# Expert weights in longer rows and fewer transfers, and a shorter warm-up, in a macaron block's kernel

## The reference

```python
x = x + 0.5 * ffn(layernorm(x), ...)
x = x + attn(layernorm(x), ...)
x = x + 0.5 * ffn(layernorm(x), ...)

def ffn(x):                                  # 64 experts, 6 per token, F = 192, H = 512
    topk_w, topk_ids = grouped_topk(x @ gate_w, bias)
    # per expert e, the first CAP of its tokens:
    h = silu(buf[e] @ w_gate[e]) * (buf[e] @ w_up[e])
    y[tokens of e] += topk_w * (h @ w_down[e])
    return y + silu(x @ ws_gate) * (x @ ws_up) @ ws_down
```

## Time and profile before

| | |
|---|---|
| median of 3 runs | 1313.1 us (1312.18 to 1315.88) |
| profiled execution | 1316.83 us, its span 1315.0 us |
| mean granted TensorE clock | 0.964 |
| busy: TensorE, VectorE, ScalarE, GpSimd | 1199.3, 614.9, 508.3, 526.3 us |
| moved by DMA | 288.73 MB in 180,972 packets |
| of that q1 (SP's queue) | 214.73 MB in 144,928 packets, 51.2% of sixteen engines over the span |
| q0 (GpSimd's queue) | 57.69 MB in 23,808 packets, 19.3% |

### The profile page before, as it was taken

One profiled execution on the slowest core, in us unless ns is written; L12 is line 12 of the kernel. 1 busy time (PEld: TensorE's weight loads), 2 busy tenths in 40 slices (PEclk: granted clock), 3 DMA queues, 4 the chain that ended last, 5 costly groups with the idle time before them and its releaser, 6 DMA issues.

```text
span 1315.0 us, 26511 instructions
## 1 busy us (share of the span) xinstructions
PE 1199.3 (91%) x10352; PEld 789.8 (60%) x10352; DVE 614.9 (47%) x1198; ACT 508.3 (39%) x1303; POOL 526.3 (40%) x417
## 2 busy tenths in 40 slices
PE   7998999999779889999999999999999999998770
PEld 5535777776557655665565565564437777776650
DVE  7791222222125677777777866643790222221120
ACT  2222111111113467888788778761122111111100
POOL 0113655555531654443434433100104555655533
PEclk9998999999999889999999999999999999999895
DMA  9989999999988533233423342230959999999977
GB/s 335 396 277 295 322 322 319 315 308 322 308 230 243 159 87 76 66 81 81 125 70 81 107 103 66 81 141 37 370 190 341 320 322 321 315 311 311 314 179 134
DMA packets 180972, 288.73 MB, mean 220 GB/s; under 512 B 21488, under 2 KB 103792, under 8 KB 180848
## 3 DMA queue, kind: packets, MB, share of 16 engines
q1 hardware_dynamic: 144928, 214.73, 51.2%
q0 software_dynamic: 23808, 57.69, 19.3%
q10 hardware_dynamic: 12112, 14.61, 3.2%
HBM read 210.15 MB, written 55.57 MB: 202 GB/s over the span
## 4 chain that ended last, share of the span: by engine, by line
PE 61%; DVE 13%; DMA 12%; issue 5%; ACT 4%; POOL 2%; SPq 1%; ACTq 0%; DVEq 0%; POOLq 0%
PE ps L386 15%; PE ps L402 9%; PE ps L462 5%; PE ps L504 4%; PE ps L516 4%; PE ps L482 4%; DMA out<-osb,tok 4%; DMA ya_d<-osb,tok 3%; DMA buf<-xn_d,tok 3%; PE ps L530 3%; PE ps L369 2%; PE ps L444 2%; PE ps L285 2%; PE ps L572 2%; DVE Mx L1200 2%
## 5 line engine op out<-in xcount | busy, mean ns | idle before, releaser
L386 PE MATMUL ps<-bufT,gu 128*64 128x96 f32 x6144 | 296.6, 258 | 20.0 <-issue 17.4
L386 PEld LDWEIGHTS ps<-bufT,gu 128*64 128x64 f32 x6144 | 286.6, 175 | 29.1 <-issue 18.3
L1200 DVE TENSOR_REDUCE Mx<-ps 128x1 f32<-128x512 f32 x256 | 170.8, 684 | 70.9 <-PE ps L482 64.6
L791 ACT ACTIVATE ps<-ps,Mx 128x512 f32<-128x512 f32 x256 | 175.4, 687 | 49.3 <-DVE Mx L1200 42.9
L402 PE MATMUL ps<-wd,h 64*96 64x512 f32 x768 | 182.5, 608 | 8.6 <-DVE osb L1113 8.3
L747 ACT COPY bufT<-ps 128x384 f32<-128x384 f32 x128 | 60.5, 477 | 312.7 <-PE ps L369 312.5
L806 ACT ACTIVATE PT<-ps 128x512 f32<-128x512 f32 x256 | 159.2, 623 | 50.7 <-PE ps L504 48.4
L1103 DVE TENSOR_TENSOR h<-sg,ps 128x288 f32<-128x288 f32 x64 | 29.1, 454 | 312.1 <-PE ps L386 312.1
L1347 POOL DMA_INDIRECT buf<-xn_d,tok x128 | 130.0, 1015 | 100.4 <-issue 57.5
L1113 DVE TENSOR_SCALAR osb<-ps,gt 96x512 f32<-96x512 f32 x128 | 89.9, 742 | 144.5 <-PE ps L402 144.5
L482 PE MATMUL ps<-St 96*128 96x512 f32 x252 | 117.3, 484 | 7.7 <-ACT ps L791 7.7
(11 more groups left out here) (162 smaller groups left out, 1685.2 us busy)
## 6 DMA issues: line engine op xcount, KB each, us to landing
gu<-in_L_ffn_w_gate SPq DMA_DIRECT2D x128, 384.0 KB, 10.2
gu<-in_L_ffn_w_up SPq DMA_DIRECT2D x128, 384.0 KB, 12.0
wd<-in_L_ffn_w_down SPq DMA_DIRECT2D x192, 256.0 KB, 10.5
St<-HL SPq DMA_DIRECT2D x186, 128.0 KB, 2.4
qkr<-in_L_attn_W_in SPq DMA_DIRECT2D x28, 256.0 KB, 3.4
X<-in_L_attn_X SPq DMA_DIRECT2D x4, 1024.0 KB, 11.2
ya_d<-X SPq DMA_DIRECT2D x4, 1024.0 KB, 18.2
yb_d<-XN ACTq DMA_DIRECT2D x16, 256.0 KB, 2.6
```

The source lines that it names most:

```text
L386: t = e.matmul(bk[64 * k:64 * k + 64, CAP * j:CAP * j + CAP], gu[:, 2 * k + m, c, j:F:3], f.bufT[(2 * q + k) % 4][:, c, :], start=(c == 0) ...
L791: e.activation(bk, bk, ACT.Exp, bias=Mx[:, qt, hl:hl + 1], accum_out=Dn[:, qt, hl:hl + 1]).then_inc(a_den, 1)
L1200: e.tensor_reduce(Mx[:, qt, hl:hl + 1], bank((4, 5, 7)[n % 3]), AX, ALU.max, negate=True).then_inc(a_max, 1)
```

## The change

`load_up` issues two transfers per pair in place of four, each of 256 rows of 3072 bytes in place of 1536. `load_down` issues one in place of three, of 128 rows of 6144 bytes in place of 2048. The counts of the two waits follow. `pe_busy` at the attention's head does 34 products in place of 45.

```diff
         def pe_gate_up(e, f, q):
-            e.wait_ge(s_gu[q % NR], loaded(f, 2 * q, 4))
+            e.wait_ge(s_gu[q % NR], loaded(f, 2 * q, 2))
         def pe_down(e, f, q):
-            e.wait_ge(s_dn[q % NR], loaded(f, 2 * q, 3))
+            e.wait_ge(s_dn[q % NR], loaded(f, 2 * q, 1))
             pe_experts(e, f1)
             e.wait_ge(f_h, E // 2)
-            pe_busy(e, 45)
+            pe_busy(e, 34)
         def load_up(e, f, q):
             gu = f.ring[q % NR][0]
             x = slice(2 * q, 2 * q + 2)
-            for c in (slice(0, 2), slice(2, 4)):
-                for m, w in enumerate((w_gate, w_up)):
-                    e.dma_start(gu[:, m::2, c, :], w[x].rearrange("x (p c) f -> p x c f", c=4)[:, :, c, :]).then_inc(s_gu[q % NR], 16)
+            for m, w in enumerate((w_gate, w_up)):
+                e.dma_start(gu[:, m::2, :, :], w[x].rearrange("x (p c) f -> p x c f", c=4)).then_inc(s_gu[q % NR], 16)
         def load_down(e, f, q):
-            for j in range(3):
-                e.dma_start(wd[:, j, :], w_down[x].rearrange("x (p j) h -> (x p) j h", j=3)[:, j, :]).then_inc(s_dn[q % NR], 16)
+            e.dma_start(wd[:, :, :], w_down[x].rearrange("x (p j) h -> (x p) j h", j=3)).then_inc(s_dn[q % NR], 16)
```

## The result

The changed kernel takes 1330.73 us (median of 4 runs, 1329.15 to 1333.52) against 1312.64 (4 runs, 1310.34 to 1315.88): ratio 1.0122, 95% interval 1.0102 to 1.0142. It is 1.2% **slower**; the prediction had said 1299 us and faster. (The quotient of the two medians is 1.0138. The ratios here are those on record, with their intervals.) The profiled execution took 1331.35 us, its span is 1329.5 against 1315.0 before.

A forecast was written before the change was run, and what follows sets the result against it. Bound: full DMA engines, with weight reloads and serial scatters both slower than TensorE. Gains of 7 us (first FFN), 4 (second) and 3 (warm-up), 14 off 1316.8, give 1303, less 3.7 for the median: 1299 us, range 1281 to 1331.

The forecast's parts named there:

- Both loops: In the FFNs: weight reloads, 10.6 us a pair to become 10.2, and GpSimd's serial scatters, about 8.6 us each.
- the late weights: Last gate/up products start 15.4 us late in the first FFN, 19.9 in the second; the second has 11.0 us of weight waits.
- ScalarE's wait: End of first FFN: 13.6 us waiting for the attention's first weights, expected to be gone.
- case A: The prediction's own case: weights gain, scatters lose, the loops trade; 1294 to 1306 us, chance 0.38.
- the lap: Time from one scatter's issue to the next: from about 8.6 us to 8.95; over 9.3 would be wrong.
- the row of turns: Each of a scatter's six rows per engine cedes to one weight row, 76 ns becoming 150: +0.45 us per lap.
- The second term: Before the experts: larger rows may delay ScalarE's stores and the first gathers, half a microsecond each.
- The free last laps: End of each FFN, loads over: the last scatters follow at 5.0 us each, to 391 and 1274 us.
- Warm-up: Attention's head: eleven fewer products gain 3 us, low bound 0; first cast 15 us behind the last scatter's landing.
- D: Rival, slower: a scatter's start waits behind weight rows in flight, lap 9.8 to 10.5; centre 1330 us, chance 0.28.
- B: Rival: turns are not by row, scatter laps stay 8.6 us; 1287 us, chance 0.20.
- C: Rival: nothing measurable, longer laps eat the weights' gain or rows are cut again; 1309 to 1317 us, chance 0.14.

The follow-up runs named there:

- w34: Kernel before with 34 warm-up products in place of 45 and nothing else: 1310.94 us, ratio 0.9981.
- down_one_short: Kernel before with down weights in one 768 KB transfer, rows still 2048 bytes, in six (second FFN five) of eight ring buffers: 1311.06 us, ratio 0.9994.
- gu_long: Kernel before with only gate and up weights in 3072-byte rows and two transfers: 1313.5 us, ratio 1.0000.
- both_mid: Kernel before with gate and up rows of 3072 bytes and down rows of 4096 and 2048 bytes: 1312.96 us, ratio 0.9994.
- down_long: Kernel before with only down weights changed, one transfer with 6144-byte rows: 1333.91 us, ratio 1.0137.
- after_start: Changed kernel with the short rows of before for the first eight pairs of each FFN: 1326.10 us, ratio 1.0100.
- down_long_i2: Kernel before with down weights in 6144-byte rows, two transfers each filling every second partition: 1325.35 us, ratio 1.0086.
- half: Kernel before with 34 warm-up products and gate and up rows of 3072 bytes from pair 16 on, down rows 2048: 1307.24 us, ratio 0.9958.

## Why the prediction was wrong

**What bounds the kernel**: right in its parts. Both loops are there, the weights' and the scatters', and the change did make the first faster and the second slower. SP was free early, the late weights and ScalarE's wait were gone, q1's packets came out to the last one, and the mean weight row was the 150 ns forecast. The time of 1330.7 us lies at the very end of the range, 1331, which the rivals had stretched so far; case A's own ended at 1306.

**The step that failed is the lap.** "I take a lap of 8.95"; measured 9.44 and 9.33, past the 9.3 that the prediction had named as its sign of being wrong. The term was sized at +0.45 us for six turns, less 0.1; it is +0.82 and +0.75. The prediction's own chain carries it to the result. Scatter 25 starts at 373.51 where 355.6 was forecast: 4.8 us are the first scatter's, 13 the 25 laps'. Pair 30 stands 14.0 us behind it, at 387.46 (13.5 forecast), and pair 31 7.2 behind that, at 394.63 (8 less 3 forecast). The last scatter follows 13.8 us later, at 408.45 where 391 stood. The second FFN repeats it: its first scatter 7.7 us late, 9.8 more by scatter 25 at 1255.97, and the last gate/up at 1278.84 where 1257 was forecast.

Why the lap was too small: the row of turns took a scatter as six turns, each the mean weight row, and left the time before its first row as it was. The single records of q0 in the traces (start and duration of each row; means of 17 laps in each FFN) show both parts. In three kernels with short rows (before, w34, down_one_short) the first row of a scatter is served 4.9 to 5.1 us after its issue and the last one 1.6 to 1.8 later; in the changed kernel it is 5.3 and 5.4, and then 2.1. A row of a scatter takes 176 ns in both kernels, so what grew is the time before and between them, 0.2 to 0.5 us of it before the first. The two queues from 1.6 to 4.7 us after the issue of a scatter, first the one of the earlier trace rows, then the changed kernel's at 249.50, show one thing that differs there: q0 is still busy with gathers issued earlier.

```profile
q1 hardware_dynamic: 660, 1.01, 96.0%
q0 software_dynamic: 30, 0.06, 7.5%
...
q1 hardware_dynamic: 152, 0.58, 62.8%
q0 software_dynamic: 105, 0.34, 38.6%
```

How much of the later start that is, is not shown. The 0.3 to 0.5 us within the six turns look like the forecast, but that is luck: in gu_long and both_mid, with mean rows of 111 and 129 ns, this part stays at 1.7 to 1.8, and in down_long, with 91, it is 1.9. The lap does not follow the mean row. It does follow the row's length, and 6144 bytes stand out. That the prediction chose the middle of an unknown cost by a rule that one stretch of 1536- and 2048-byte rows showed, and applied it to rows three times as long, is its error. Whether turns are by row, by packet or otherwise is still open.

**The second term is the start.** "Larger rows may delay ScalarE's stores and the first gathers, half a microsecond each"; the first scatter starts at 136.6 where six kernels with short rows at the start have 131.8 to 134.4, so 2 to 5 us, and after_start puts its worth at some 4 us, with the uncertainty said there.

**The free last laps** were counted nearly right, 21.2 us from scatter 27 to the last where 20 were forecast, but they came after a longer loop. Of what the loads gained nothing is left once the scatters set the pace.

**Warm-up**: right. The head's first cast stands 15.3 us behind the last landing. The chain of waits at the changed kernel's head (start us, us, what):

```profile
410.38 4.23 DMA yb_d<-osb,tok
...
429.94 0.44 DVE xT L1156
```

410.38 + 4.23 = 414.6, and 429.94 follows 15.3 later. Alone it is worth 0.2%, 2 to 3 us, at the edge of what was measured.

**The rivals.** D had the sign, 1330 and "it decides from a lap of about 9.3 on", and the laps were 9.33 and 9.44. Its mechanism, a start that waits behind a number of rows, asked for 3 us more before the first row and a lap of 9.8 at least. The start did grow, but by 0.2 to 0.5 us, so that its 1330 met the 1330.7 is luck. B fell: laps did not stay at 8.6. Its ground does not carry it either, for a turn of so many rows takes longer with longer rows; only a turn of so many bytes would have kept the lap. C's words "laps of 9.1 to 9.2 eat what the weights give" put the edge too high: gu_long at 8.95 stands even, down_long_i2 at 9.18 and 9.17 loses 0.9%.

## What to carry to other kernels

When a bulk load shares its DMA engines with small transfers in a serial loop, price a longer row by that loop, not by the load's own rate: here rows up to 4096 bytes cost between nothing and 0.3% and 6144-byte rows 1.4%, though the load itself became faster. Where two loops both run close to the bound, what one gains the other can lose, so look for where each of them binds in time. Splitting the change there (short rows while the scatter loop has the lead to keep, long ones once weights are late) lost nothing in `half`; that it gains is not shown. Don't load one half of the partitions at a time: it cost 8 to 10%.

## What the runs showed of the hardware

Not expected were: transfers to one half of the partitions at 280 GB/s against 322 for the kernel before, over 120 to 230 us, while every second partition with short rows cost nothing; a lap of scatters that rises by 0.6 us for 6144-byte rows in 128 of 1152 rows of a pair, and by 0.3 for rows of 3072 and 4096 bytes throughout; ScalarE's stores at 8.4 us in place of 6.6 beside long rows of another queue; and a pause of TensorE in the midst of a product, 0.65 us a pair, that comes in nearly every pair once scatters are gone, and for which the profile names no cause.
